# Products of the identity that nothing reads, set into TensorE's waits in the fills of both attention layers and at the first layer's end

## The reference

```python
x = x + _L0_cond_ref(x, cond_2048, L0_cond_Wq, L0_cond_Wo)      # attention, 8 heads of 32, q = k = v
x = x + _L1_cond_ref(x, cond_2048[:, None, :])                  # causal depthwise convolution, 16 taps
x = x + _L2_cond_ref(cond_2048, x, L2_cond_W_ih, L2_cond_W_hh, L2_cond_b_ih, L2_cond_b_hh)   # GRU, 256 steps
x = x + _L3_cond_ref(x, cond_2048, L3_cond_Wq, L3_cond_Wk, L3_cond_Wv, L3_cond_b)            # attention, 16 heads of 16
```

```python
q = xt @ Wq.T
scores = scale * jnp.einsum('bhqd,bhkd->bhqk', qh, qh)
logits = (scores * cmask + (1.0 - cmask) * NEG) * rmask
attn = jax.nn.softmax(logits, axis=-1)
ctx = jnp.einsum('bhqk,bhkd->bhqd', attn, qh)
out = ctx @ Wo.T
```

## Time and profile before

| | |
|---|---|
| median of 3 runs | 2847.83 us (2840.78 to 2853.43) |
| the profiled execution's own time | 2837.42 us |
| its span in the trace | 2835.6 us |
| PE busy | 2601.0 us, 92% of the span |
| DVE busy | 2114.8 us, 75% |
| ACT busy | 1340.7 us, 47% |
| mean granted PE clock over the span | 0.973 |

### The profile page before, as it was taken

The page is one execution under the profiler, slowest core; times in us unless marked ns, Lnnn a source line. Parts: engine busy times, 40 slices in busy tenths (PEclk is TensorE's granted clock), DMA queues, the critical chain, the costliest instruction groups (busy, mean ns, idle before and its releaser), DMA issues. The chain is left out here.

```text
span 2835.6 us, 113854 instructions
## 1 busy us (share of the span) xinstructions
PE 2601.0 (92%) x46640; PEld 1476.2 (52%) x46640; DVE 2114.8 (75%) x4262; ACT 1340.7 (47%) x2346; POOL 883.2 (31%) x838
## 2 busy tenths in 40 slices
PE   6999999999779999999999999995999999999987
PEld 2233333333269998988888989981222222222221
DVE  4666667666768888888888888755777777777775
ACT  1555555555322222222222222221778788888877
POOL 0444444444412221112111111112234434444343
PEclk7999999999789999999999999997999999999999
DMA  1311101101100000000000000003434444444532
GB/s 43 116 49 33 53 29 51 53 27 43 28 21 0 0 1 1 0 0 0 0 0 0 0 1 0 0 1 84 97 92 107 120 98 114 117 97 114 120 91 54
DMA packets 121516, 131.65 MB, mean 46 GB/s; under 512 B 32224, under 2 KB 85368, under 8 KB 121362
## 3 DMA queue, kind: packets, MB, share of 16 engines
q1 hardware_dynamic: 115630, 123.70, 16.9%
q10 hardware_dynamic: 5760, 6.56, 0.9%
HBM read 85.83 MB, written 44.34 MB: 46 GB/s over the span
## 5 line engine op out<-in xcount | busy, mean ns | idle before, releaser
L873 PE MATMUL exp_ps<-region,gru_hT 128*16 128x128 f32 x16384 | 498.5, 274 | 44.7 <-DVE gru_hT L1000 14.0
L1544 DVE TENSOR_REDUCE x<-exp_ps 128x2 f32<-128x1024 f32 x352 | 426.3, 1222 | 103.5 <-PE exp_ps L1650 102.0
L873 PEld LDWEIGHTS exp_ps<-region,gru_hT 128*16 128x16 f32 x16384 | 428.3, 103 | 113.1 <-DVE gru_hT L1000 113.1
L402 POOL TENSOR_TENSOR l_probs<-l_probs 128x1024 f32<-128x1024 f32 x128 | 311.4, 2447 | 321.3 <-ACT l_probs L478 225.1
L1470 ACT ACTIVATE region<-exp_ps,x 128x1024 f32<-128x1024 f32 x336 | 370.2, 1110 | 79.0 <-PE exp_ps L1623 79.0
L804 POOL TENSOR_TENSOR xT<-xT,gru_hT 128x64 f32 (+1 forms) x256 | 120.0, 469 | 889.6 <-DVE gru_hT L1000 881.0
L918 ACT ACTIVATE gru_r<-exp_ps 128x128 f32<-128x128 f32 x256 | 71.0, 277 | 582.9 <-PE exp_ps L873 582.9
L958 DVE SCALAR_TENSOR_TENSOR xT<-x,condT,xT (+1 forms) x420 | 318.5, 800 | 0.1
L575 DVE TENSOR_REDUCE l_maxes<-exp_ps 128x2 f32<-128x1024 f32 x176 | 214.7, 1222 | 131.5 <-PE exp_ps L641 129.2
L858 PE MATMUL exp_ps<-region,gru_x_st 128*32 128x128 f32 x8192 | 271.7, 274 | 12.9 <-POOL gru_hT L825 12.9
L1636 PE MATMUL bank<-region,x 128*17 128x512 f32 x2048 | 272.0, 603 | 6.7 <-ACT region L1470 3.6
(11 more groups left out here) (176 smaller groups left out, 4077.7 us busy)
## 6 DMA issues: line engine op xcount, KB each, us to landing
region<-key_query_scratch SPq DMA_DIRECT2D x128, 192.0 KB
key_query_scratch<-x SPq DMA_DIRECT2D x48, 256.0 KB, 2.4
key_query_scratch<-region SPq DMA_DIRECT2D x48, 256.0 KB, 2.6
region<-in_x SPq DMA_DIRECT2D x16, 512.0 KB, 4.4
l_rden<-rden_scratch SPq DMA_DIRECT2D x128, 64.0 KB, 2.0
l_xres<-in_x SPq DMA_DIRECT2D x16, 512.0 KB, 3.7
x_scratch<-x SPq DMA_DIRECT2D x16, 512.0 KB, 2.8
l_rden<-rden_scratch SPq DMA_DIRECT2D x240, 32.0 KB, 1.8
```

Source lines behind the costliest of these rows:

```text
L402: pool.tensor_tensor(probs[:, first, :, :], probs[:, first, :, :], probs[:, second, :, :], ALU.add).then_inc(added, 1)
L873: last = pe.matmul(out[QW * j:QW * j + rows, cols], hT[:, p, k, state], group_of(wh[:, k, gate, :], j), start=False, stop=True, skip_group ...
L1544: dve.tensor_reduce(maxes[:, half, qt, head % HH:head % HH + 2], pairs[ring.place[2 * slot + 1]][:, :, :], AX_X, ALU.max).then_inc(taken[" ...
```

## The change

A helper `keep_busy` issues n products of the identity with itself, 128x128 f32, into a bank that nothing reads then. In the first layer: 12 ahead of the wait for the weights, 3 ahead of the wait for their copies, 2 in each of the 16 slots of step -1, and 56 in slot 15 of step 16, behind a wait for `o_taken` and ahead of the last "out". In the second layer: 8, 8 and 16 around the small products of the setup, and 48 in step -1 ahead of the first maxima's wait for the stack. That is 103 products in the first layer and 80 in the second. Nothing else changes on any engine.

```diff
+def keep_busy(pe, g, out, n):
+
+    for _ in range(n):
+        pe.matmul(out[:, 0:P], g.ident[:, :], g.ident[:, :], start=True, stop=True)
...
+            keep_busy(pe, g, o_ps, 12)
             pe.wait_ge(w_loaded, 32)
...
                 last.then_inc(w_turned, 1)
+            keep_busy(pe, g, o_ps, 3)
             pe.wait_ge(w_taken, 2)
...
                     products(s, par, slot)
+                    if isinstance(s, int) and s == -1:
+
+                        keep_busy(pe, g, o_ps, 2)
+                    if isinstance(s, int) and s > LAST and slot == AT["out"]:
+                        pe.wait_ge(o_taken, 2 * B)
+                        keep_busy(pe, g, o_ps, 56)
...
                 last.then_inc(w_turned, 1)
+            keep_busy(pe, g, g.bank[4], 8)
             pe.wait_ge(cols_ready, 3)
...
             pe.transpose(g.bank[3][0:1, P:P + 8], tops[:, 0:1], g.ident[0:8, 0:8]).then_inc(tops_turned, 1)
+            keep_busy(pe, g, g.bank[4], 8)
             pe.wait_ge(bound_ready, 1)
             pe.matmul(g.bank[3][:, 2 * P:2 * P + 4], one_row[:, :], bound[:, 0:4], start=True, stop=True).then_inc(spread_ready, 1)
+            keep_busy(pe, g, g.bank[4], 16)
             pe.wait_ge(factors_ready, 1)
...
+                if isinstance(s, int) and s == -1 and tile == 0:
+                    keep_busy(pe, g, g.bank[4], 48)
                 if tile % 16 == 0:
                     wait(pe, stack_loaded[2 * h // HH], 16 * LOADS * (s + off + 1))
```

## The result

The changed kernel takes 2837.48 us, the median of 15 runs (2825.86 to 2845.8), against 2843.64 us for 15 runs of the kernel before: a ratio of 0.9967, 95% interval 0.9952 to 0.9981. That is 6.2 us by the medians, 9.4 us by the ratio: a real gain, within the 0.5% that was called no change. The forecast was 2837.4 us, from 2847.8 us and a gain of 10.4. The kernel before now measured 4.2 us less than those 2847.8, so the time was met with a gain smaller than forecast. The changed kernel's profiled execution took 2838.24 us with a span of 2836.3 us, 0.7 us longer than the one before, and that is what has to be explained.

The account below looks back on a forecast made before the run. TensorE's clock, low where layers meet, and PE and DVE taking turns in the fill were taken as the bound. Terms -5.2 - 2.2 - 3.0 = -10.4 us from 2847.8 gave 2837.4 us, range 2827 to 2852.

Parts of the forecast that it names:

- First layer's fill, -5.2 us: First layer up to 69 us: half of a possible 12.9 us saved by a higher clock, less 1.2 for added products.
- Does the level hold?: Whether the clock stays high through the first layer's fill; the forecast let it save half of 12.9 us.
- The price of 1.2 us for the slots' products: First layer's step -1: two products a slot, 0.44 us a pair, mostly hidden in PE's waits; bounds 0.5 and 7.0 us.
- the sum for that case: First layer's fill with the clock high throughout: -12.9 + 1.2 = -11.7 us.
- First layer's end, -2.2: Last output projection of the first layer: starting warm takes 4.6 instead of 7.4 us; -2.8 + 0.6.
- The allowance of 0.6: First layer's end: the 56 products might finish late, 1.0 us behind the context; about half of that was taken.
- Second layer's start, -3.0: Second layer's setup: x transposes and first projection faster by 2.7 us, plus 0.3 in the fill of step -1.
- All hidden at the high level: Second layer's start: the second 8, the 16 and the 48 products fit in waits of 2.11, 4.30 and 13.03 us.
- In between, nothing has new work ... what comes earlier stays earlier: Between the changed places, the GRU and steady steps keep their order, so time won earlier is kept.
- Products of the identity don't raise the level: Rival, everywhere products were added: all cost 0.43 us, +29 us in sum, 2877 us; chance 0.10.
- The level holds: Rival: the clock stays high through all fills, -18.1 us in sum, 2829.7 us; chance 0.25.
- No gain in the fill: Rival: the clock falls in the fill as before, only the ends win, -2.6 us, 2845 us; chance 0.15.

Follow-up runs that it names:

- second comparison: The changed kernel run once more, unedited, against the kernel before: ten runs, five from 2816.3 to 2821.8 us, five from 2829.5 to 2838.3; ratio 0.994 (0.9916 to 0.9965).

## Why the prediction was right, and where it was not

- **First layer's fill, -5.2 us: right, by a mixture.** Six traces of kernels with this fill have step 2 at 138.3 to 143.9 us, mean 141.6; four without (before twice, and the two with no product ahead) at 145.2 to 149.0, mean 147.3: -5.8. "Does the level hold?" was answered with half; it held wholly in one of the six (the taps two to a slot) and up to about 55 us in two more, and fell and rose earlier in the other three. The price of 1.2 us for the slots' products was too low in what it rested on: a pair costs 0.64 us between maxima, not 0.44, and fills PE to 1.70 us a slot. What the high level wins in the slots they eat, all but 1 to 2 us. Where the level held wholly, step 2 came 9.1 us ahead of that mean of 147.3, not the 11.7 of the sum for that case.
- **First layer's end, -2.2: right as a mean, of two values.** The projection took 4.5 to 4.6 us in eight of the eleven traces with products ahead of it, and 6.2 to 6.3 us, with a low clock in it, in three (one product a slot, the taps two to a slot, the transposes), 5.0 in the mean. The three traces without the products took 7.4, 6.9 and 7.3 us: -2.2. The allowance of 0.6 for products that end late was not needed: with 56 of them they ended ahead of the context, 1.7 us ahead of the projection in the trace of the change. That the low level could come back behind them the forecast had not counted.
- **Second layer's start, -3.0: right in the mean.** From the layer's first instruction to its first exponential, 76.3 us is the mean of the ten traces with products (identity products, all but the transposes' run), 78.7 that of the three without: -2.4. With the transposes it is 78.2. The single traces lie from 74.3 to 77.8 and from 77.6 to 80.0, and the change's own has only 0.4 us. "All hidden at the high level" left out the first 8 products, which ran partly at the low one and held the next transpose for 0.4 us there.
- **"In between, nothing has new work ... what comes earlier stays earlier": wrong.** Step 15 has no new work, but took 61.0, about 47 or 40.8 us by where the clock stood in it and which additions the taps then held up. The trace of the change has the long one, that of before the short one; that takes back 11.8 us and makes the two spans equal. The forecast's sum stood against a median that mixes both. That the forecast of 2837.4 met 2837.5 was luck in good part: the kernel before came out 4.2 us below the 2847.8, a median of three runs, that the sum started from, and the gain by the medians was 6.2 us, not 10.4. The mix of lengths moves such a median as well: in the recorded comparison 12 of 15 runs of the change lie in the slower group, in the next one 5 of 10.
- **The rivals.** "Products of the identity don't raise the level" is out: the clock rose at 11.0 us in the middle of them. "The level holds" has one trace wholly and two nearly, and none that wins the full 12.9 less 1.2 in the fill. "No gain in the fill" has none.

The sum of the three terms as measured, means over traces, is -5.8 - 2.2 - 2.4 = -10.4 us; between groups of a kind the second comparison gives 15 us. The 4.6 us between them are open, and so is whether the change shifts the odds of the long step: 12 of 15 and 5 of 10 against 11 of 25.

## What to carry to other kernels

Products that nobody reads are worth their place where an engine idles in one piece and a dense stretch follows on the path: a few microseconds each, 2.2 and 2.4 here, as long as they end before what the engine waits for; beyond that each one costs its full time. Between short dependent pieces they fill the engine themselves and give almost nothing. When two traces differ by more than the change can explain, look for a stretch that has two lengths, compare it by itself, and try whether holding the clock there removes the slow one. Here it narrowed the spread from 23 us to 11 and 5 but won nothing over the changed kernel, since the fastest runs went with the slowest. And one trace of a kernel is one draw: the changed kernel's own shows a layer gaining 0.4 us where ten traces show 2.4.

## What the hardware showed that was not expected

An addition on GpSimd (128x1024 f32, 2.3 us alone) that starts within a row of DVE taps (128x448 f32, 0.6 us each, one behind the other) can be held to the row's end: 15.6, 12.5 and 10.1 us were seen, each ending 2.2 us behind the row, and with most of the taps left out 2.8 at most. It can also go the other way: in six traces an addition that started during the eighth of nine taps took 2.75 us, in one of these the additions that started during the sixth and eighth of 27 took 2.9 and 2.7, and the tap behind each start took 2.8 instead of 0.7. And 24 f32 transposes raise the clock as products do.
